# Second pass of a wavelet mixing kernel: smaller matmul tiles, two copies of the spread images, six places

## The chip, the cores and the metric

One Trainium2 chip, one core. The metric is the device time of the kernel in microseconds, lower is better. The kernel before takes 1980.73 us, the median of three runs.

## The reference

The input x is 8 batches of 32 channels, 256 images of 512x512 in float32. Each image is taken through a four-level wavelet analysis with symmetric padding. At the last level the low band and the three detail bands are 42x42 coefficients each; their channels are mixed, one 32x32 matrix for every coefficient, and the image is put together again. Only the last level is changed by the mix:

```
yl, yh = _dwt2(x, 4)
yl_out = einsum('bixy,ioxy->boxy', yl, w_yl)
yh_out = yh[:-1] + [einsum('bicxy,iocxy->bocxy', yh[-1], w_yh)]
return _idwt2(yl_out, yh_out)
```

Since the other levels come back as they were, the output is x plus the synthesis of the change in the 84x84 last-level coefficients (2 bands per axis, BANDS, of 42, COEFS; ROWS is 84). The kernel computes that.

## The kernel before, in words

**Pass 1** (to about 664 us) reads all 256 images, 1 MB each, on SyncE's queue (L325 to L333, eight slots) and brings each to 84x84 coefficients: TensorE along the height in 32x32 tiles (`h_stage`, L419), then a turn, then along the width. **The mix** (to about 739 us) goes over 32 pieces of weights (`mix`, L505 and L510, weights in a ring of four, L342); VectorE and ScalarE build its operands. In every four pieces TensorE also turns one step of the mixed coefficients of the last batch back, coefficients on partitions (`first_coefs`, L519), and ScalarE copies them to `delta` (`copy_delta`, L699).

**Pass 2** reads each image again, adds the synthesis of its delta and stores it. For an image ScalarE copies its 84x84 deltas to `pick` (L746); TensorE multiplies them with the width synthesis (the spread, L549, K=84 of 128 rows used, 512 columns, two records per float32 matmul); ScalarE copies the result to one of four `spread` buffers (L758); TensorE multiplies that with the height synthesis into PSUM banks 2 to 5 (the out stage, L565 for single images, L578 for pairs; four row sets k, each pair matmul 128 rows by 64 columns of the array and 512 long); VectorE adds PSUM to x in two halves (L854). TensorE waits for the add of the previous image's same half (`added`), and the add waits for `o_done`. The first 16 images, still on chip or loaded early, go singly; the other 240 as 120 pairs of 2 MB.

Three queues order pass 2. GpSimd's issues the loads (L302): a pair is loaded into place k of seven (`PLACES`, 2 MB each) once the pair stored from it has landed (`pair_stored`). SyncE's issues the stores in order (L370, L373, L377) once the adds are done. TensorE's order is written out: in `turn2` (eight images) the spread of image c+2 goes ahead of the out stage of image c. In every fourth `turn2`, seven times in all, the coefficients of the next batch are turned (`coefs_stage`, L539) between images, after ScalarE has staged them (`copy_stage`, L734) and before it copies them (`copy_delta`). The last pair is loaded and stored in pieces (L318, L380, L384).

## Time and profile before

| | |
|---|---|
| median of three runs | 1980.73 us (1978.71 to 1983.08) |
| the profiled execution | 1983.0 us, span 1981.1 us |
| TensorE matmul busy | 1899.7 us (96%) |
| VectorE, ScalarE, GpSimd busy | 825.3, 486.1, 72.7 us |
| moved | 558.29 MB read, 268.44 MB written, mean 418 GB/s |
| TensorE's granted clock, mean | 0.994 of full |

The span is what the profile of one core shows from its first to its last instruction. Busy shares are means over stages with different limits, and a busy TensorE is not one at its peak. DMA share is the mean busy share of the 16 DMA engines; it comes out a little above 1 where all 16 always have a packet.

### The profile page before, as it was taken

The numbers are of one execution on the slowest core, as the hardware profiler recorded it, in microseconds if no ns is written. First come the engines' busy times: TensorE is split into PE (matmuls) and PEld (weight loads), VectorE is DVE, ScalarE is ACT, GpSimd is POOL, SyncE is SP. The second block draws the span as 40 slices with busy tenths as digits, with TensorE's granted clock in tenths as the row PEclk, the third lists the DMA queues.
The fourth block names the chain that finished last, engine by engine and source line by source line (L and its number), as shares of the span: only waits on it lengthen the run. The fifth ranks groups of instructions, "written<-read, shape, count | busy, mean of one in ns | idle before, by whom it ended". The sixth has DMA issues, their size and how long they took to land.

```text
span 1981.1 us, 47583 instructions
## 1 busy us (share of the span) xinstructions
PE 1899.7 (96%) x19625; PEld 825.6 (42%) x19625; DVE 825.3 (42%) x931; ACT 486.1 (25%) x1060; POOL 72.7 (4%) x130
## 2 busy tenths in 40 slices
PE   8999999999999899999999999999999999999995
PEld 4666666666666554332232232232232232222221
DVE  2222222222222345555545555555545445445442
ACT  2233232332332551121121131121121121121110
POOL 1000000000000000000000000000000000000000
PEclk9999999999999999999999999999999999999998
DMA  9999999999999899999999999999999999999997
GB/s 383 405 408 414 412 422 421 421 422 422 422 422 422 338 406 381 420 421 430 429 430 429 431 429 431 430 431 430 430 429 429 430 431 431 430 431 431 430 432 303
DMA packets 80233, 827.12 MB, mean 418 GB/s; under 512 B 8912, under 2 KB 8912, under 8 KB 13520
## 3 DMA queue, kind: packets, MB, share of 16 engines
q1 hardware_dynamic: 62784, 575.10, 69.5%
q0 software_dynamic: 17424, 251.67, 29.9%
q8 instruction: 18, 0.29, 0.1%
q14 instruction: 7, 0.06, 0.0%
HBM read 558.29 MB, written 268.44 MB: 417 GB/s over the span
## 4 chain that ended last, share of the span: by engine, by line
PE 59%; DMA 36%; issue 2%; SPq 1%; DVE 1%; ACT 0%; DVEq 0%; POOLq 0%; ACTq 0%; POOL 0%
PE ps L578 27%; DMA x_sb<-x 19%; DMA out<-x_sb 16%; PE ps L419 10%; PE ps L549 8%; PE ps L432 5%; PE ps L565 3%; PE ps L510 1%; PE ps L505 1%; SPq L333 1%; PE ps L443 1%; DVE x_sb L854 1%; PE ps L451 1%; PE ps L539 1%; PE ps L465 1%
## 5 line engine op out<-in xcount | busy, mean ns | idle before, releaser
L854 DVE TENSOR_TENSOR x_sb<-ps,x_sb 128x1024 f32<-128x1024 f32 x292 | 354.9, 1223 | 348.4 <-PE ps L578 228.0
L578 PE MATMUL ps<-spread_sb,const 128*64 128x512 f32 x1920 | 438.9, 599 | 11.5 <-DVE x_sb L854 6.5
L578 PE MATMUL ps<-work,const 128*64 128x512 f32 x1920 | 438.9, 599 | 10.5 <-DVE x_sb L854 5.5
L854 DVE TENSOR_TENSOR work<-ps,work 128x1024 f32<-128x1024 f32 x220 | 267.3, 1223 | 255.9 <-PE ps L578 159.1
L419 PE MATMUL ps<-x_sb,const 32*32 32x512 f32 x8192 | 288.9, 601 | 23.1 <-DMA x_sb<-x 19.7
L549 PE MATMUL ps<-const,pick 128*84 128x512 f32 x514 | 277.1, 621 | 0.0
L432 PEld LDWEIGHTS ps<-const,work 128*128 128x128 f32 x2048 | 244.8, 192 | 51.8 <-ACT work L621 37.6
L578 PEld LDWEIGHTS ps<-spread_sb,const 128*64 128x64 f32 x1920 | 128.9, 138 | 312.8 <-issue 275.3
L578 PEld LDWEIGHTS ps<-work,const 128*64 128x64 f32 x1920 | 129.4, 139 | 311.3 <-issue 276.6
L432 PE MATMUL ps<-const,work 128*128 128x84 f32 x2048 | 253.9, 276 | 0.0
L621 ACT COPY work<-ps 128x512 f32<-128x512 f32 x256 | 131.4, 600 | 419.3 <-PE ps L419 419.3
L813 DVE COPY work<-ps 128x336 f32<-128x336 f32 x256 | 129.9, 507 | 151.2 <-PE ps L432 151.2
L419 PEld LDWEIGHTS ps<-x_sb,const 32*32 32x32 f32 x8192 | 138.8, 103 | 124.2 <-issue 85.0
L819 DVE COPY work<-ps 128x336 f32<-128x336 f32 x65 | 33.0, 507 | 342.0 <-PE ps L443 342.0
L758 ACT COPY spread_sb<-ps 84x512 f32<-84x512 f32 x121 | 70.3, 581 | 425.6 <-PE ps L549 424.8
L758 ACT COPY work<-ps 84x512 f32<-84x512 f32 x120 | 69.8, 581 | 417.1 <-PE ps L549 416.6
L549 PEld LDWEIGHTS ps<-const,pick 128*84 128x84 f32 x514 | 59.9, 151 | 185.8 <-issue 185.5
L302 POOL DMA_DIRECT2D x_sb<-x x68 | 36.2, 532 | 1383.2 <-DMA out<-x_sb 1383.2
L746 ACT COPY pick<-work 84x84 f32 (+1 forms) x258 | 67.3, 261 | 12.9 <-issue 10.4
L839 DVE COPY work<-mix_sb 32x448 f32<-32x448 f32 (+1 forms) x96 | 36.4, 379 | 37.4 <-PE ps L510 32.3
L443 PE MATMUL ps<-work,const 128*32 128x336 f32 x520 | 50.2, 458 | 0.6 <-DVE work L813 0.6
L451 PE MATMUL ps<-work,const 128*84 128x336 f32 x130 | 47.6, 448 | 0.6 <-DVE work L819 0.6
(46 smaller groups left out, 529.9 us busy)
## 6 DMA issues: line engine op xcount, KB each, us to landing
x_sb<-x SPq DMA_DIRECT2D x256, 1024.0 KB, 10.1
x_sb<-x POOLq DMA_DIRECT2D x68, 2048.0 KB, 16.5
out<-x_sb SPq DMA_DIRECT2D x68, 2048.0 KB, 38.2
work<-x POOLq DMA_DIRECT2D x51, 2048.0 KB, 16.5
out<-work SPq DMA_DIRECT2D x51, 2048.0 KB, 36.0
work<-w_full SPq DMA_DIRECT2D x30, 896.0 KB, 7.5
out<-x_sb SPq DMA_DIRECT2D x9, 1024.0 KB, 7.4
work<-x SPq DMA_DIRECT2D x8, 1024.0 KB, 6.3
```

What stands on the lines that cost most here:

```text
L419: last = nc.tensor.matmul(ps[to:to + TILE, m], const[part, A3H + TILE * r:A3H + TILE * r + TILE], x_sb[part, GROUP * a + m, r], start=r == ...
L432: last = nc.tensor.matmul(ps[:, 4 + m % 2, ROWS * k:ROWS * k + ROWS], along_h[:, m, P * k:P * k + P], const[:, A4 + ROWS * m:A4 + ROWS * ( ...
L443: last = nc.tensor.matmul(ps[TILE * k:TILE * k + TILE, 6, 0:GROUP * ROWS], const[:, at:at + TILE], turned[:, k].rearrange("p m r -> p (m r ...
L451: nc.tensor.matmul(ps[0:ROWS, 7, 0:GROUP * ROWS], const[:, A4:A4 + ROWS], third, start=True, stop=True).then_inc(c_done, 1)
L549: nc.tensor.matmul(ps[0:ROWS, p], pick[:, p], const[:, SW:SW + SIZE], start=True, stop=True).then_inc(s_done[p], 1)
L565: last = nc.tensor.matmul(ps[:, 2 + k], const[:, SH + P * k:SH + P * k + P], spread(c), start=True, stop=True)
L578: last = nc.tensor.matmul(ps[64 * h:64 * h + 64, 2 + k], const[:, SH + P * k + u:SH + P * k + P:2], spread(c - u + h), start=True, stop=True)
L621: nc.scalar.copy(along_h[:, m], ps[:, m]).then_inc(h_copied, 1)
L746: nc.scalar.copy(pick[0:ROWS, p], delta[0:ROWS, o]).then_inc(picked[p], 1)
L758: nc.scalar.copy(spread(c)[0:ROWS], ps[0:ROWS, p]).then_inc(s_copied[p], 1)
L813: nc.vector.tensor_copy(turned[:, :, m], ps[:, 4 + m % 2, 0:SEGS * ROWS].rearrange("p (k r) -> p k r", k=SEGS),).then_inc(t_copied, 1)
L854: nc.vector.tensor_tensor(part, ps[:, 2 + 2 * half:4 + 2 * half], part, ALU.add).then_inc(added[half], 1)
```

## The change

The synthesis of one half of an axis needs only 32 of the 42 coefficients of each band, so both products of pass 2 are cut in halves with K = 64. The spread of an image becomes 8 matmuls of 64x64 tiles, 256 columns each, into two PSUM banks; it is laid out twice, with the halves of the height on partitions 0 to 63 and 64 to 127 in both orders, and ScalarE copies both arrangements (eight buffers of 512 columns). The out stage of a pair image becomes 16 matmuls of 64x32 tiles, 512 long, the tiles of even and odd k on opposite rows of the array; of a single image 8 of 64x64. `pick` is written in two copies. A step of coefficients is turned by 8 matmuls without transpose mode in place of 4 with it, interleaved by band (`by_band`). The spread constants shrink from 1024 columns to 512. The places go from seven to six, and pass 2 is looped over groups of four images, `fours`. Turning the next batch now lies within one group of four, each step behind waits for the copies ahead of it. The cut diff (VectorE's loop over the places, SyncE's and the rest of ScalarE's group loop follow the same pattern and are left out):

```diff
-PLACES = 7
+PLACES = 6
 PAIRS = IMAGES // 2 - SLOTS
-ROUNDS2 = PAIRS // PLACES
-assert PAIRS == PLACES * ROUNDS2 + 1
+ROUNDS2 = PAIRS // PLACES - 1
+
+FOURS_BATCH = CHANNELS // GROUP
+FOURS = IMAGES // GROUP
+SINGLE = 2 * SLOTS // GROUP
+
+WINDOW, SHIFT = 32, COEFS - 32
...
-SW, SH, EYE, NEG = 592, 1104, 1616, 1744
+SW, SH, EYE, NEG = 592, 848, 1104, 1232
...
-    c[:ROWS, SW:SW + SIZE] = back.T
-    for r in range(ROW_RUN):
-        c[:ROWS, SH + P * r:SH + P * r + P] = back[r::ROW_RUN].T
+
+    windows = [[COEFS * b + SHIFT * h + j for j in range(WINDOW) for b in range(BANDS)] for h in range(2)]
+    for h in range(2):
+        part = slice(64 * h, 64 * h + 64)
+        half = back[SIZE // 2 * h:SIZE // 2 * (h + 1)]
+        assert np.abs(np.delete(half, windows[h], axis=1)).max() == 0
+        c[part, SW:SW + SIZE // 2] = half[:, windows[h]].T
+        for r in range(ROW_RUN):
+            of = h ^ (r % 2)
+            c[part, SH + 64 * r:SH + 64 * r + 64] = back[P * ROW_RUN // 2 * of + r:P * ROW_RUN // 2 * (of + 1):ROW_RUN, windows[of]].T
...
-        pick = sb("pick", [P, 2, ROWS])
-        spread_sb = sb("spread_sb", [P, 2, SIZE])
+        pick = sb("pick", [P, 2, P])
...
-        place += [work[:, e:e + 2 * IMAGE].rearrange("p (r w) -> p r w", w=SIZE) for e in (0, AT_W, AT_W + 2 * IMAGE)]
-
...
+        spreads = [AT_EARLY - SIZE] + [AT_EARLY + IMAGE + SIZE * e for e in range(6)]
+        assert max(at, AT_W + IMAGE * (EARLY - 3)) <= spreads[0]
+        spreads = [const[:, SW - SIZE:SW]] + [work[:, e:e + SIZE] for e in spreads]
...
-        def spread(c):
-
-            return spread_sb[:, c % 4] if c % 4 < 2 else more_spread[:, c % 4 - 2]
+        def spread(c, a):
+
+            return spreads[7 - (2 * (c % 4) + a)]
+
+        def by_band(step):
+
+            return step.rearrange("p (q j b) -> p q b j", q=Q, b=BANDS)
+
+        def window(rows, h):
+
+            return rows.rearrange("p (b r) -> p b r", b=BANDS)[:, :, SHIFT * h:SHIFT * h + WINDOW]
...
-            for k, e in ((4, 0), (5, 3), (6, 5)):
+            for k, e in ((4, 0), (5, 3)):
...
-            pool.wait_ge(pair_stored[0], 16 * ROUNDS2)
+            for k in range(PLACES - 1):
+                pool.wait_ge(pair_stored[k], 16 * ROUNDS2)
+                load_pair(k, PLACES * ROUNDS2 + k)
+            pool.wait_ge(pair_stored[PLACES - 1], 16 * ROUNDS2)
             for u in range(2):
-                pool.dma_start(place[0][:, 4 * u:4 * u + 4], x_pairs[0, :, 4 * u:4 * u + 4]).then_inc(last_loaded[u], 16)
+                rows = slice(4 * u, 4 * u + 4)
...
+            def turn_step(step, bank):
+
+                for q in range(Q):
+                    for h in range(2):
+                        last = nc.tensor.matmul(ps[64 * h:64 * h + 64, bank, P * q:P * q + P],
+                                                step[:, ROWS * q + 2 * SHIFT * h:ROWS * q + 2 * (SHIFT * h + WINDOW)],
+                                                const[:, EYE:EYE + P], start=True, stop=True)
+                return last
...
+            def coefs_stage(c, g, k):
+
+                pe.wait_ge(s_copied[c % 2], 2 * g + (c + 2) // 2 + 2)
+                for v in (2 * c, 2 * c + 1):
+                    pe.wait_ge(staged, STEPS * (k - 1) + v + 1)
+                    pe.sem_inc(d_begun, 1)
+                    turn_step(stage[:, v], 6 * (c % 2) + v % 2).then_inc(d_done, 1)
+
+            def spread_rows(p, of):
+
+                for a in range(2):
+                    for half in range(2):
+                        to = 64 * (half ^ a)
+                        for h in range(2):
+                            part = slice(64 * h, 64 * h + 64)
+                            last = nc.tensor.matmul(ps[to:to + 64, 6 * p + h, 256 * a:256 * a + 256], of(part, half),
+                                                    const[part, SW:SW + 256], start=True, stop=True)
+                last.then_inc(s_done[p], 1)
+
...
+                pe.sem_inc(s_begun, 1)
+                spread_rows(p, lambda part, half: pick[part, p, 64 * half:64 * half + 64])
+
+            def out_stage(c, g):
+
+                p, n = c % 2, GROUP * g + c
+                pe.wait_ge(s_copied[p], 2 * g + c // 2 + 2)
+                for two in range(2):
+                    pe.wait_ge(added[two], n + 1)
+                    pe.sem_inc(o_begun[two], 1)
+                    for k in (2 * two, 2 * two + 1):
+                        for half in range(2):
+                            at = 64 * (half ^ (k % 2))
+                            last = nc.tensor.matmul(ps[64 * half:64 * half + 64, 2 + k],
+                                                    const[at:at + 64, SH + 64 * k:SH + 64 * k + 64],
+                                                    spread(c, k % 2)[at:at + 64], start=True, stop=True)
+                    last.then_inc(o_done[two], 1)
+
+            def pair_stage(c, g):
+
+                u, n = c % 2, GROUP * g + c
                 for h in range(2):
-                    pe.wait_ge(s_copied[h], SLOTS // 2 * t + c // 2 + 2)
-                for half in range(2):
-                    pe.wait_ge(added[half], n + 1)
-                    for k in (2 * half, 2 * half + 1):
+                    pe.wait_ge(s_copied[h], 2 * g + c // 2 + 2)
+                for two in range(2):
+                    pe.wait_ge(added[two], n + 1)
+                    pe.sem_inc(o_begun[two], 1)
+                    for k in (2 * two, 2 * two + 1):
                         for h in range(2):
-                            last = nc.tensor.matmul(ps[64 * h:64 * h + 64, 2 + k], const[:, SH + P * k + u:SH + P * k + P:2],
-                                                    spread(c - u + h), start=True, stop=True)
-                    last.then_inc(o_done[half], 1)
-
-            def turn2(t, batch=None):
-
-                for c in range(SLOTS):
-                    if c < SLOTS - 2:
-                        spread_stage(c + 2, t)
+                            for half in range(2):
+                                at, to = 64 * (half ^ (k % 2)), 64 * h + 32 * half
+                                last = nc.tensor.matmul(ps[to:to + 32, 2 + k],
+                                                        const[at:at + 64, SH + 64 * k + u:SH + 64 * k + 64:2],
+                                                        spread(c - u + h, k % 2)[at:at + 64], start=True, stop=True)
+                    last.then_inc(o_done[two], 1)
...
+            def fours(g, batch=None):
+
+                for c in range(GROUP):
+                    if batch is not None and c >= 2:
+
+                        pe.wait_ge(d_copied, STEPS * batch + IDLE + 1 + 2 * (c - 1))
+                    if c < GROUP - 2:
+                        spread_stage(c + 2, g)
                     else:
+                        spread_stage(c + 2 - GROUP, g + 1)
+                    pair_stage(c, g)
+                    if batch is not None and c < STEPS // 2:
+                        coefs_stage(c, g, batch)
+                if batch is not None:
+                    pe.wait_ge(d_copied, STEPS * (batch + 1) + IDLE + 1)
+                    pe.sem_inc(d_begun, 1)
+
+            pe.wait_ge(cleared, 3)
+            spread_stage(0, 0)
+            with pe.Fori(0, SINGLE) as g:
+                for c in range(GROUP):
+                    if c < GROUP - 1:
+                        spread_stage(c + 1, g)
+                    else:
+                        spread_stage(0, g + 1)
+                    out_stage(c, g)
+            spread_stage(1, SINGLE)
+            with pe.Fori(SINGLE, FOURS_BATCH - 2) as g:
+                fours(g)
+            with pe.Fori(0, BATCH - 1) as k:
+                fours(FOURS_BATCH * k + (FOURS_BATCH - 2), batch=k + 1)
+                with pe.Fori(0, FOURS_BATCH - 1) as r:
+                    fours(FOURS_BATCH * k + r + (FOURS_BATCH - 1))
+            with pe.Fori(FOURS - 2, FOURS) as g:
+                fours(g)
...
+            def pick_image(c, g, single=False):
+
+                p, n = c % 2, 2 * g + c // 2
+                if single:
+                    o = CHANNELS - SLOTS - SLOTS * (g >> 1) + GROUP * (g & 1) + c
+                else:
+                    o = APART * ((g >> 3) & 1) + (CHANNELS - 2 - 2 * (c // 2) + c % 2) - GROUP * (g & (FOURS_BATCH - 1))
                 act.wait_ge(s_done[p], n)
+                for half in range(2):
+                    last = nc.scalar.copy(pick[:, p, 64 * half:64 * half + 64].rearrange("p (j b) -> p b j", b=BANDS),
+                                          window(delta[:, o], half))
+                last.then_inc(picked[p], 1)
+
+            def copy_spread(c, g, done):
+
+                p, n = c % 2, 2 * g + c // 2
                 act.wait_ge(s_done[p], n + 1)
+                act.wait_ge(o_done[1], done)
+                for a in range(2):
+                    last = nc.scalar.copy(spread(c, a).rearrange("p (h w) -> p h w", h=2),
+                                          ps[:, 6 * p:6 * p + 2, 256 * a:256 * a + 256])
+                last.then_inc(s_copied[p], 1)
+
+            def copy_spread_pair(c, g):
+                copy_spread(c, g, GROUP * g + (2 * (c // 2) - 1))
+
...
+            def fours(g, batch=None):
+                for c in range(GROUP):
                     if batch is not None and c == 0:
+                        for e in (2, 6, 7):
+                            act.wait_ge(early_stored[e], 16)
+                    if batch is not None and 1 <= c <= STEPS // 2:
+                        copy_delta(2 * (c - 1), batch, None)
+                        copy_delta(2 * (c - 1) + 1, batch, None)
+                    if c < GROUP - 3:
+                        pick_image(c + 3, g)
                     else:
+                        pick_image(c + 3 - GROUP, g + 1)
+                    if c < GROUP - 2:
+                        copy_spread_pair(c + 2, g)
                     else:
+                        copy_spread_pair(c + 2 - GROUP, g + 1)
+                    if batch is not None and c < STEPS // 2:
                         copy_stage(2 * c, batch)
                         copy_stage(2 * c + 1, batch)
+                if batch is not None:
+                    act.wait_ge(d_copied, STEPS * (batch + 1) + IDLE + 1)
```

## Rows read from the trace of the kernel before

**Rows 1.** The page: GB/s moved by DMA in 40 equal slices of 49.5 us.
```profile
GB/s 383 405 408 414 412 422 421 421 422 422 422 422 422 338 406 381 420 421 430 429 430 429 431 429 431 430 431 430 430 429 429 430 431 431 430 431 431 430 432 303
```
**Rows 2.** Windows: length, busy of PE, PEld, DVE, ACT, POOL, clock, DMA share, GB/s.
```profile
655.00:690.00 35.00, 28.94 (x1281) 20.43 (x1280) 15.34 (x39) 21.38 (x41) 0.00 (x0) 1.00 0.85 305
690.00:735.00 45.00, 42.26 (x2438) 27.75 (x2425) 23.36 (x61) 26.26 (x47) 0.00 (x0) 1.00 1.01 416
...
750.00:755.00 5.00, 5.00 (x13) 2.05 (x12) 2.75 (x3) 0.74 (x2) 0.00 (x0) 1.00 0.88 369
755.00:760.00 5.00, 5.00 (x13) 2.14 (x12) 3.16 (x3) 0.89 (x3) 0.66 (x1) 1.00 0.74 262
760.00:765.00 5.00, 5.00 (x13) 2.21 (x12) 2.67 (x3) 1.33 (x4) 0.00 (x0) 1.00 1.02 316
765.00:770.00 5.00, 5.00 (x13) 2.07 (x12) 2.45 (x2) 0.74 (x2) 0.00 (x1) 1.00 0.91 383
...
850.00:1500.00 650.00, 650.00 (x2616) 192.71 (x2614) 337.50 (x276) 140.99 (x337) 34.94 (x66) 1.00 1.01 430
1500.00:1950.00 450.00, 428.02 (x1693) 123.45 (x1689) 219.90 (x183) 84.04 (x206) 24.36 (x46) 1.00 1.01 431
```
**Rows 3.** Timeline, late in pass 2: start, length, engine, line, shapes, records [idle before <-releaser].
```profile
1512.41 3.66 PE L578 MATMUL ps<-spread_sb,const 128*64 128x512 f32 x16 [0.60 <-DVE work L854]
...
1516.00 1.09 PE L549 MATMUL ps<-const,pick 128*84 128x512 f32 x2
...
1520.99 2.35 DVE L854 TENSOR_TENSOR work<-ps,work 128x1024 f32<-128x1024 f32 x2 [3.65 <-DMA work<-x]
```
**Rows 4.** Groups by line and shape: records | busy us, mean ns | idle before.
```profile
L854 DVE TENSOR_TENSOR x_sb<-ps,x_sb 128x1024 f32<-128x1024 f32 x292 | 354.9, 1223 | 348.4 <-PE ps L578 228.0 <-DMA x_sb<-x 98.4 <-PE ps L565 22.0
...
L758 ACT COPY spread_sb<-ps 84x512 f32<-84x512 f32 x121 | 70.3, 581 | 425.6 <-PE ps L549 424.8
...
L746 ACT COPY pick<-work 84x84 f32 x224 | 58.5, 261 | 12.8 <-issue 10.4
...
L734 ACT COPY work<-mix_sb 128x336 f32 x36 | 27.2, 806 | 0.0
...
L699 ACT COPY work<-ps 84x512 f32 x30 | 16.3, 583 | 35.5 <-PE ps L539 35.0
```
**Rows 5.** Timeline in pass 1: two groups of 64 matmuls on 16 tiles.
```profile
79.42 4.46 PE L419 MATMUL ps<-x_sb,const 32*32 32x512 f32 x128 [0.46 <-DMA x_sb<-x]
...
90.50 5.96 PE L419 MATMUL ps<-x_sb,const 32*32 32x512 f32 x128 [1.61 <-DMA x_sb<-x]
```
**Rows 6.** Window over the second of these groups, columns as in rows 2.
```profile
92.00:96.00 4.00, 4.00 (x100) 2.04 (x91) 0.00 (x0) 0.00 (x0) 0.00 (x0) 0.68 1.01 422
```
**Rows 7.** Timeline from the mix into pass 2: last turn of coefficients, first stores.
```profile
739.25 0.64 PE L519 MATMUL ps<-const 128*84 128x128 f32 x4 [0.30 <-ACT const L690]
...
747.37 0.34 SPq L370 DMA_DIRECT2D out<-x_sb  x1
...
751.66 4.62 SPq L370 DMA_DIRECT2D out<-x_sb  x2
```
**Rows 8.** Waits from 690 to 740 us: who waited for what, total us, times, longest.
```profile
PEld ps L510 <- DMA work<-w_full: 12.2, 21, 1.2
```
**Rows 9.** The page's DMA issues: count, KB each, median us to landing.
```profile
x_sb<-x POOLq DMA_DIRECT2D x68, 2048.0 KB, 16.5
out<-x_sb SPq DMA_DIRECT2D x68, 2048.0 KB, 38.2
...
const<-consts SPq DMA_DIRECT2D x1, 592.0 KB, 12.2
```
**Rows 10.** The chain of waits at the end: start, length, what.
```profile
1892.45 45.14 DMA out<-x_sb
...
1938.55 21.36 DMA x_sb<-x
```
**Rows 11.** Window over the last stores, columns as in rows 2.
```profile
1967.00:1979.00 12.00, 0.00 (x0) 0.00 (x0) 0.00 (x0) 0.00 (x0) 0.00 (x0) 0.50 0.07 31
```

194 lines of the change are left out of this document (68 added, 126 removed).

## The prediction

> **What bounds the kernel now.** I read the slices first. TensorE is over 90% busy nearly everywhere, but so are the DMA engines, and their rate is the flatter of the two: 429 to 431 GB/s in every slice from about 900 us to 1930 us, 421 to 422 in pass 1, with one hole, 338, where pass 1 ends, and a shallow one, 381, where pass 2 begins [rows 1]. The windows then separate the two. From 850 to 1500 us TensorE is busy the whole time, from 1500 to 1950 it is idle 22 of 450 us, waiting through VectorE for loads; the DMA share is 1.01 in both and the rate 430 and 431 GB/s [rows 2]. So TensorE's being full or not makes no difference to what is moved. The chain of waits names the out stage for a large part of the span, but only because a full engine is never seen to wait. A pair is 2 MB in and 2 MB out, 4.19 MB, which at 431 GB/s is 9.73 us. TensorE needs 3.66 us for the out stage and about 1.0 for the spread, 4.7 an image and 9.3 a pair [rows 3], a little less than DMA: it is behind when pass 2 begins and has caught up by 1500 us.
>
> What a faster TensorE can win is thus only time in which DMA engines stand idle. There are three such places. From 655 to 690 us the share is 0.85: 5.3 us. From 750 to 770 us it is 0.88, 0.74, 1.02, 0.91 in four windows of 5 us, 0.12 + 0.26 + 0.09 = 0.47 of one, 2.35 us. By the rate (369, 262, 316, 383 against 430) it is (61 + 168 + 114 + 47) / 430 x 5 = 4.5 us [rows 2]. The third is the end: from 1967 to 1979 us the share is 0.07, one engine of sixteen (1/16 is 0.0625), still working through its stores [rows 11]. No matmul runs there, and the chain of the end is store 45.1 us, load 21.4 us, add, last store [rows 10].
>
> **The change part by part.**
>
> *The out stage and the spread.* Now 8 matmuls go two at a time in 3.66 us, 0.915 us for each round [rows 3]. In pass 1, 64 matmuls as long go sixteen at a time in 4.46 us, 1.115 us a round [rows 5]; there too four tiles of different rows write the same partitions in different banks, the pattern of the new code. The new out stage has 16 matmuls on eight tiles: two rounds, between 1.83 and 2.23 us. I take 2.0. The spread, 8 matmuls half as long on four tiles, is two rounds of half the length, 0.92 to 1.12, say 1.0. An image costs TensorE 3.0 us instead of 4.7, a pair 6.0 (5.5 to 6.7). VectorE's two adds of 1.22 us, 2.45 us an image [rows 4], and ScalarE's copies, 2 x 0.58 + 2 x 0.26 = 1.7 us instead of 0.84 [rows 4], both fit under it. All of it lies under the 9.73 us of DMA, so for the 120 pairs its worth is 0. The extra semaphore increments of TensorE lie there too.
>
> *The start of pass 2.* Single images now leave every 4.3 us (747.37 to 751.66) [rows 7], the 1 MB stores alone ask for 244 GB/s, and the loads of pairs only come once two stores have landed: that is the hole. With 3.0 us an image the stores ask for 350 GB/s. The first store comes later, however: the last turn of coefficients takes some 0.5 us more, image 0 needs its two picks (0.52), its spread is copied twice (0.58 more), and its first half out is shorter by 1.83 - 1.0 = 0.8. Instead of at 747.4 us [rows 7] it is issued at about 748.2, the second 3.0 us after it (4.3 now), and so on: by the eighth it is 8 us ahead of now. Up to about 752 DMA has early loads left, so the late start is covered. From then the stores and, from about 757, the loads fill it. Gain: between 0 and the 4.5 us of lost rate; I take the idle share, 2.3 us.
>
> *Turning coefficients in the mix.* Four matmuls take 0.64 us [rows 7]. Eight matmuls of 128 columns, each in two records and two at a time, are four rounds of a quarter of 0.915, 0.92 us at least; without overlap they are eight such rounds, 1.83. I take 1.15, 0.5 more, nine times. From 690 to 740 us TensorE waited for weights in 21 pieces, 12.2 us in all [rows 8], 2.3 us in four pieces, so the 0.5 there is hidden (at most 1.2, hidden as well). From 655 to 690 us DMA is not full, and two turns lie on the path: 1.0 us lost, 2.4 at most, 0 if ScalarE's copies end last there. The copies written with a stride of two elements read with a stride of eight as before (0.81 us); I cost them at nothing, as ScalarE was only 26 of 45 us busy [rows 2].
>
> *Constants.* The second load of constants was 592 KB [rows 9] for 1184 columns; 672 remain, 336 KB. 0.26 MB at 420 GB/s is 0.6 us of pass 1, where DMA is full. GpSimd's two memsets fewer are off the path.
>
> *Six places instead of seven.* In the cycle of a place the load takes 16.5 us and the store 38.2 to landing [rows 9], 54.7 us, or 5.6 pairs at 9.73 us: that many of the seven are in DMA's hands and the rest wait for or are in the adds. With six and a TensorE that no longer lags, about 0.6 of a place is with the engines and 5.4 in DMA. A transfer's own time at full rate is 4.9 us, so the queues are deep waits, not needed ones. Cost 0; what covers it is that depth. The slow sixteenth of DMA is the only thing that eats it: late in the run the store takes 45.1 us [rows 10]. GpSimd's queue waits for `pair_stored` as now and has nothing else behind; SyncE's stores keep their order.
>
> *The next batch's coefficients.* Seven times, within four images, ScalarE has 6 x 0.81 + 6 x 0.58 us more [rows 4] and TensorE six turns of 1.15. Were all serial, each image would take 4.5 + 5.3 = 9.8 us, the group 39 us against 19.5 of DMA: the adds fall 19.5 us behind, two pairs. 5.4 - 2 = 3.4 places are still in DMA. Cost 0 to 14 us (the rival below); I take 0, and TensorE regains 3.7 us a pair.
>
> *The end.* The last load still goes when a store has landed; the same two adds and last stores follow. 0.
>
> Sum: -2.3 - 0.6 + 1.0 = -1.9 us. The trace's own execution took 1983.0 us, 2.3 above the median of 1980.7, so it gives 1981.1 there and **1978.8 us** as a median. The bounds of the terms give -4.5 - 0.6 = -5.1 and 2.4 - 0.6 = +1.8.
>
> **The clock.** In pass 1 TensorE was idle for 1.6 us ahead of one group of 64 matmuls, the window over that group shows the clock at 0.68 in the mean, part of it at 1.2 GHz, and the group took 5.96 us instead of 4.46 [rows 5, 6]. Late in pass 2 it idles 0.6 us a pair at 2.4 GHz [rows 2, 3]; after the change it idles 9.7 - 6.0 = 3.7 us a pair. At half clock an image costs 6.0 us. With half of its work at 1.2 GHz a pair takes 9.0 us, still under 9.73, and the sum stays. With all of it there, 12.0, the kernel would be 2.3 us a pair slower; the threshold is 62% of the work at the low level, and an engine which is that full has been granted 2.4 GHz in this trace [rows 2]. The Trainium skill, "TensorE: Matmul & The Clock Gate", section "HAM oscillation — how this bites in real kernels", speaks against the change: matmuls in bursts with waits for DMA between them fall back to the low clock each time. By the row I expect this partly and at no cost.
>
> **The rivals.**
> - *The slow DMA engine is let go* (faster). One engine ends some 12 us after the rest [rows 11]. If its lag came from competition with fifteen full ones, six places would hold those back and it would catch up: up to 12 us less, 1967 to 1975, say 1971. For it: the lag is there. Against: when alone it moves 31 GB/s for the core, no more than a sixteenth of 431 (27) and a little. Chance 0.09.
> - *TensorE bounded after all until 1500 us* (faster). Then DMA would rise above 430 GB/s; 1% over 650 us is 6.5 us, 1974. Against: 430 with TensorE full, 431 with it waiting. Chance 0.05.
> - *Six places run dry at the next batch's coefficients* (slower). The group of four is the most serial part, and the slow engine's late landings (45.1 us instead of 38.2) take another 0.7 place. It decides from when the adds are some three pairs, 29 us, behind. At 2 us dry in each of seven places it is +14, 1993. Against: the estimate is 19.5 us with nothing overlapped. Chance 0.09.
> - *Tiles on different rows don't run at once, or the clock stays low* (slower). Four rounds for the out stage as now and 1.83 for the spread make 11.0 us a pair, 1.3 over DMA, 120 times: +150. Pass 1's sixteen tiles speak against it. Chance 0.03.
> - *The change doesn't do what it says*: the hole at 750 us stays, since landings and not issues space the loads there. 1981. Chance 0.08.
>
> **How the numbers follow.** The forecast has 0.66. About 0.2%, 4 us, is what a measurement of this kernel can tell from none: faster means under 1976.8, slower over 1984.7. Three runs scattered by 4.4 us, so a forecast of -1.9 with bounds -5.1 to +1.8 comes out faster in some 0.22 of its cases and slower in 0.04. Faster: 0.66 x 0.22 + 0.09 + 0.05 = 0.28. Slower: 0.66 x 0.04 + 0.09 + 0.03, rounded to 0.15. Same: 0.57. The range reaches from 1971.5, half of the slow-engine case, to 1985.5, the upper bound with scatter; left out are the slower cases and the other half, under 0.2.
>
> **What would show it.** TensorE's busy time in pass 2 near 3.0 us an image, VectorE then waiting for loads from about 900 us on instead of 1500, DMA share 1.01 and 430 GB/s from 760 to 1950 us as before, the windows from 750 to 770 us at 1.0, those from 655 to 690 a little lower than 0.85. I am wrong if a window after 850 us falls under 0.98, or if the last engine's tail is gone.

## The result, and the profile after

The changed kernel takes 2013.5 us (median of 4 runs, 2011.1 to 2017.1) against 1980.5 us before (1978.7 to 1983.1): 1.0167 times as long, 95% interval 1.0155 to 1.018. The forecast was 1978.8 us, no change. (The 1980.73 us ahead of the prediction was the median of the first three of the four runs before.) The profiled spans are 2015.3 and 1981.1 us, 34.2 apart.

Of the page of the changed kernel, its engines and the slices of 50.4 us, against [rows 1]:
```profile
span 2015.3 us, 65865 instructions
...
PE 1648.0 (82%) x27817; PEld 798.5 (40%) x27817; DVE 812.5 (40%) x931; ACT 644.9 (32%) x1579; POOL 71.1 (4%) x128
...
PEclk9999999999999999888988888888798888888787
DMA  9999999999999899999999999999999999999997
GB/s 382 413 413 421 419 421 422 422 422 422 422 422 421 328 397 417 426 430 431 430 430 426 424 427 420 407 395 403 405 415 405 410 409 411 414 402 411 409 414 294
```
TensorE is less busy, the DMA engines are as busy as before, and yet they move less: 430 GB/s until about 1050 us as before, then 420 to 427 and from about 1260 us 395 to 415. The changed kernel also executes 65865 instructions where the one before has 47583.

Its windows, columns as in [rows 2]:
```profile
655.00:690.00 35.00, 28.79 (x1343) 20.50 (x1344) 15.46 (x40) 20.01 (x38) 0.00 (x0) 1.00 0.82 292
...
750.00:755.00 5.00, 5.00 (x64) 2.41 (x60) 4.34 (x5) 2.39 (x8) 0.00 (x0) 1.00 1.01 423
755.00:760.00 5.00, 5.00 (x64) 2.40 (x59) 4.61 (x4) 2.38 (x8) 0.66 (x1) 1.00 1.00 359
760.00:765.00 5.00, 5.00 (x68) 2.54 (x64) 4.50 (x4) 2.38 (x9) 0.53 (x1) 1.00 0.99 403
765.00:770.00 5.00, 4.96 (x67) 2.40 (x63) 4.26 (x5) 2.63 (x8) 0.00 (x0) 1.00 1.03 434
...
850.00:1500.00 650.00, 484.62 (x6520) 162.33 (x6512) 305.19 (x256) 204.88 (x560) 33.94 (x64) 0.86 1.00 419
1500.00:1950.00 450.00, 328.75 (x4436) 109.55 (x4432) 209.93 (x178) 135.25 (x376) 23.34 (x44) 0.85 1.00 409
```
The hole at 750 us is filled, as forecast. The loss is below it: at 419 instead of 430 GB/s 650 us lose 650 x 11/430 = 16.6 us, at 409 instead of 431 450 us lose 23.0; 39.6 us in all, of which the gains below give some back. DMA's share is 1.00 in both windows (0.98 from 1300 to 1400 us), so hardly anything is seen to wait: the same transfers take longer.

The timeline of the changed kernel, late in pass 2, against [rows 3]: a spread, then an out stage at each of the clock's two levels.
```profile
1509.06 1.09 PE L584 MATMUL ps<-const,pick 64*64 64x256 f32 x16
...
1510.09 1.95 PE L623 MATMUL ps<-work,const 64*32 64x512 f32 x32
...
1517.11 3.67 PE L623 MATMUL ps<-work,const 64*32 64x512 f32 x32 [4.05 <-DVE x_sb L924]
```
The DMA issues on its page, against [rows 9]:
```profile
x_sb<-x POOLq DMA_DIRECT2D x80, 2048.0 KB, 22.1
out<-x_sb SPq DMA_DIRECT2D x80, 2048.0 KB, 32.0
```
Load and store together are 54.1 us from issue to landing (54.7 before), but of six places now, not of seven: six pairs at the 9.73 us of before are 58.4 us, and 4.3 us of slack are left of 13.4.

The DMA view of two windows of 4 us of the changed kernel, its two large queues (q0 GpSimd's with the loads of pairs, q1 SyncE's with the stores; packets, MB, share of 16 engines). From 1504 to 1508 us:
```profile
q1 hardware_dynamic: 95, 1.56, 105.0%
q0 software_dynamic: 7, 0.07, 3.9%
```
From 1509 to 1513 us:
```profile
q0 software_dynamic: 92, 1.51, 96.6%
q1 hardware_dynamic: 10, 0.08, 4.9%
```
The same view of the kernel before, 1500 to 1505 us:
```profile
q0 software_dynamic: 70, 1.11, 52.0%
q1 hardware_dynamic: 68, 1.05, 49.0%
```
Loads and stores used to be mixed at every moment; now they come in turns. In the trace's DMA records a 16 KB packet took 0.611 us in the mean of 1600 to 1900 us before and 0.641 after, 4.9% more, which is the missing rate. The turns are not shown to be what slows the packets. Take the difference between load and store packets in bins of 2 us, as a share of their sum, from 1600 to 1900 us: it is 0.12 before, 0.65 after, 0.20 in e2 below, and e2's packets took 0.629 us all the same.

**One engine falls behind.** In the trace the store of a pair has 16 landings, and I take each for one of the 16 DMA engines; where one lags, it fits the tail of [rows 11] with one sixteenth of DMA busy. I call the time between the first and the last of a pair's 16 store landings the *spread of a store*. Before, it grows from 3.8 us (at 982 us) to 28.7 (at 1948), most of it between the last landing and the others (22.0): one engine loses 24.9 us in 966, 2.6%, which ends as the 12 us of [rows 11]. After the change it grows from 9.9 us (952) to 21.5 (1195), 4.8%, and stays at 24 to 26 from about 1250 us on. The stay is where the rate falls.

The table is worked out from the traces of all kernels but e9 and e14: matmuls in pass 2 for each pair image, places, growth of the spread with its end points, the level at which it stays, and the time against the kernel before. The times of landings here, in the table and with every spread below are counted from the start of the recording, some 10 us ahead of the span's start from which windows and slices count. Each growth is from one trace.
```
run     matmuls  places  growth (us at us)                level  ratio [95% interval]
before     9       7     2.6% (3.8@982, 28.7@1948)         -     1
after     24       6     4.8% (9.9@952, 21.5@1195)         25    1.0167 [1.0155, 1.018]
e1         9       6     2.2% (3.4@972, 24.6@1917)        (25)   1.0013 [1.0003, 1.0023]
e2        24       7     5.4% (9.2@933, 31.8@1355)         36    1.0085 [1.0068, 1.0102]
e3        24       5     -                                 17    1.0123 [1.0105, 1.0142]
e4         9       7     2.9% (4.7@981, 32.3@1948)         -     1.0004 [0.9994, 1.0013]
e5         9       4     -                                  5    1.006  [1.0041, 1.008]
e6         9       7     2.7% (4.7@978, 30.5@1945)         -     0.9991 [0.9978, 1.0004]
e7        36       6     6.5% (10.3@965, 26.0@1208)        26    1.0194 [1.0163, 1.0226]
e8        24       6     5.8% (9.7@954, 23.8@1196)         26    1.0128 [1.0089, 1.0168]
e10       17       7     3.8% (3.3@979, 35.2@1815)         35    1.0052 [1.0036, 1.0069]
e11        9 +96   7     13.8% (7.9@925, 39.3@1152)        40    1.0593 [1.0573, 1.0613]
e12       24       6     5.4% (9.1@956, 22.3@1199)         26    1.0136 [1.0114, 1.0158]
e13        9 +48   7     10.6% (7.4@917, 38.6@1211)        39    1.0394 [1.0351, 1.0437]
e15       19       6     4.2% (6.8@961, 21.8@1320)         25    1.0067 [1.005, 1.0083]
e16        5       7     1.5% (5.0@981, 19.1@1941)         -     0.9978 [0.9962, 0.9994]
e17        9 +24   7     3.4% (6.6@982, 32.5@1746)         35    1.0025 [1.0011, 1.0038]
e18       19       7     3.9% (5.5@848, 24.4@1336)         36    1.0078 [1.0054, 1.0103]
(+n: n instructions more on SyncE for each pair, as the trace counts them)
```

**Where each kernel loses.** The DMA records also say how much later a kernel has moved the same bytes than the kernel before. What this delay grows by from 850 to 1950 us is the loss in the pair stage alone: 40 us in the change, 0 in e1, 18 in e2, 35 in e3, 11 in e5, 0 in e6, 36 in e7, 25 in e8, 4 in e10, 107 in e11, 30 in e12, 68 in e13, 13 in e15, 2 in e17, 13 in e18, and e16 gains 1. The rest of a difference in time arises where pass 2 begins or in the last 50 us.

### The profile page after: what moved, and what is told of

It reads as the page before. It is cut to its first block, busy times and chain, and to the rows that moved or that the text cites. A ratio compares the mean times of both kernels' runs of the same rounds, so it can differ in the third digit from the quotient of the medians.

```text
span 2015.3 us, 65865 instructions
## 1 busy us (share of the span) xinstructions
PE 1648.0 (82%) x27817; PEld 798.5 (40%) x27817; DVE 812.5 (40%) x931; ACT 644.9 (32%) x1579; POOL 71.1 (4%) x128
## 4 chain that ended last, share of the span: by engine, by line
DMA 65%; PE 27%; DVE 3%; issue 2%; SPq 1%; ACT 1%; DVEq 0%; ACTq 0%; POOLq 0%; POOL 0%
DMA x_sb<-x 31%; DMA out<-x_sb 26%; PE ps L450 10%; DMA out<-work 5%; PE ps L463 5%; DMA work<-x 4%; PE ps L623 3%; DVE x_sb L924 2%; PE ps L541 2%; PE ps L536 1%; PE ps L606 1%; PE ps L584 1%; SPq L359 1%; PE ps L474 1%; PE ps L549 1%
## 5 line engine op out<-in xcount | busy, mean ns | idle before, releaser
L623 PE MATMUL ps<-work,const 64*32 64x512 f32 x6720 | 577.9, 706 | 297.2 <-DVE x_sb L924 199.1
L924 DVE TENSOR_TENSOR x_sb<-ps,x_sb 128x1024 f32<-128x1024 f32 x336 | 400.1, 1221 | 429.8 <-DMA x_sb<-x 340.4
L810 ACT COPY work<-ps 128x512 f32<-128x512 f32 x450 | 244.8, 589 | 803.8 <-PE ps L584 802.5
L623 PEld LDWEIGHTS ps<-work,const 64*32 64x32 f32 x6720 | 122.8, 114 | 591.7 <-issue 591.6
L584 PE MATMUL ps<-const,pick 64*64 64x256 f32 x4128 | 320.1, 430 | 2.2 <-issue 2.2
L924 DVE TENSOR_TENSOR work<-ps,work 128x1024 f32<-128x1024 f32 x176 | 209.3, 1220 | 230.3 <-DMA work<-x 174.1
L623 PE MATMUL ps<-const 64*32 64x512 f32 x960 | 280.2, 698 | 0.0
L584 PEld LDWEIGHTS ps<-const,pick 64*64 64x64 f32 x4128 | 151.0, 148 | 292.3 <-issue 266.8
L676 ACT COPY work<-ps 128x512 f32<-128x512 f32 x256 | 131.4, 599 | 416.7 <-PE ps L450 416.7
L800 ACT COPY pick<-work 128x64 f32 (+1 forms) x518 | 105.2, 261 | 12.6 <-DMA out<-work 12.4
L549 PE MATMUL ps<-const,work 128*64 128x128 f32 x672 | 44.0, 286 | 13.9 <-ACT work L788 13.7
```

The lines of the kernel that those rows point to most:

```text
L549: last = nc.tensor.matmul(ps[64 * h:64 * h + 64, bank, P * q:P * q + P], step[:, ROWS * q + 2 * SHIFT * h:ROWS * q + 2 * (SHIFT * h + WIND ...
L584: last = nc.tensor.matmul(ps[to:to + 64, 6 * p + h, 256 * a:256 * a + 256], of(part, half), const[part, SW:SW + 256], start=True, stop=True)
L623: last = nc.tensor.matmul(ps[to:to + 32, 2 + k], const[at:at + 64, SH + 64 * k + u:SH + 64 * k + 64:2], spread(c - u + h, k % 2)[at:at + 6 ...
L676: nc.scalar.copy(along_h[:, m], ps[:, m]).then_inc(h_copied, 1)
L800: last = nc.scalar.copy(pick[:, p, 64 * half:64 * half + 64].rearrange("p (j b) -> p b j", b=BANDS), window(delta[:, o], half))
L810: last = nc.scalar.copy(spread(c, a).rearrange("p (h w) -> p h w", h=2), ps[:, 6 * p:6 * p + 2, 256 * a:256 * a + 256])
```

## The experiments

The letters in the expectations are the theories of the moment; each is spelled out there. A diff shows the lines that carry the edit, the rest of it is left out.

**e1, six places alone.** The kernel before with `PLACES = 6` and the last round's loads and stores as the change has them.
```diff
-PLACES = 7
+PLACES = 6
```


> The kernel before with one edit: six places for pairs in place of seven. Theory A (depth): one of the 16 DMA engines falls behind, each place is held until its last sixteenth has landed, and with six places the other fifteen run out of stores and then of loads by turns, which slows each packet; then this kernel is slower than before by 1.0 to 1.7%, 2000 to 2015 us, its DMA rate falls from 430 to about 410 GB/s somewhere after 1050 us, loads then take some 22 us and stores 32. Theory B (pace and traffic): it is the new tiles, the adds that follow each load at once, the half clock or ScalarE's doubled copies that disturb DMA; then this one stays within 0.2% of before.


1985.9 us, +0.13%. Its page:
```profile
GB/s 367 415 419 421 413 416 423 416 422 422 420 422 422 329 405 382 392 417 425 431 429 431 431 429 429 430 431 432 430 431 431 430 432 430 431 431 430 431 429 316
```
430 GB/s to the end: the number of places alone is not it. Its few us are lost where pass 2 begins: the slices from 743 to 893 us have 382, 392 and 417 GB/s, those of [rows 1] 381, 420 and 421, 3.7 us.

**e2, the new tiles with seven places** (to make room, the stage of coefficients is halved, an early image lies elsewhere, and the first 16 images use two spread buffers instead of four).
```diff
-PLACES = 6
+PLACES = 7
```


> The changed kernel with seven places (room is made by a ring of four steps for the staged coefficients, by an early image under spread buffers, and by two spread buffers in place of four for the first 16 images). Theory A (depth): 1976 to 1981 us, -0.2 to 0.0%, DMA at 430 GB/s to the end. Theory B (pace and traffic): as slow as the changed kernel, 2005 to 2015 us.


2000.5 us, +0.85%: half of the loss. Its page:
```profile
GB/s 367 412 419 421 419 422 422 422 422 422 422 422 421 305 394 416 423 425 431 428 428 427 430 428 428 428 428 424 428 424 415 418 418 414 420 420 414 421 410 272
```
The rate falls only from about 1500 us on, after the spread has reached 36 us instead of 25. With the old tiles and six places the pair stage loses nothing (e1), with the new tiles and seven places 18 us, with both changes 40.

**e3, five places.** As the change, with one place fewer.
```diff
-PLACES = 6
+PLACES = 5
```


> The changed kernel with five places. Theory A (depth): slower still than with six: the fifteen engines run dry earlier, before 900 us, and have less to do by turns; 2030 to 2100 us, and the DMA share falls under 0.98. Theory B (pace and traffic): within 0.3% of the changed kernel.


2008.9 us, less than with six. The level is 17 us, reached about 1130 us. So the levels go 17, 25, 36 with five, six, seven places, about a pair's time (9.7 us) apart, but the loss does not grow with each place taken.

**e4, queues swapped.** Before, with the pair loads on SyncE and all stores of pass 2 on GpSimd.
```diff
-                    pool.wait_ge(pair_stored[k], 16 * i)
-                    load_pair(k, PLACES * i + k)
+                    pool.wait_ge(added[1], 2 * PLACES * i + (2 * SLOTS + 2 * k + 3))
+                    pool.dma_start(out_pairs[i * -PLACES + (PAIRS - 1 - k)], place[k]).then_inc(pair_stored[k], 16)
```


> The kernel before with its seven places, but in pass 2 GpSimd's queue issues all stores and SyncE's all loads of pairs. It asks where the slow sixteenth comes from. If it belongs to GpSimd's queue, the lag now shows in the stores' landings as before but more strongly, or at the loads not at all; if it belongs to one engine whatever the queue, time and the tail of some 12 us at the end stay: within 0.3% of before. If the lag goes, the tail does, and it is 8 to 12 us faster.


No change, and the spread grows by 2.9% all the same. The Trainium skill ("DMA: Bandwidth & Descriptors", section "Latency and other measured facts") says that two of the sixteen engines are usually slower and guesses at the descriptor rings of GpSimd's path. In these traces there is one, and it doesn't care which queue does what. GpSimd's queue is still in use in e4, so the guess itself is not tested.

**e5, four places.** Before, the last round as in e1.
```diff
-PLACES = 7
+PLACES = 4
```


> The kernel before with four places. Theory A2: one engine's lag can only grow as far as the places let it (stores landed 17, 25 and 36 us apart at most with five, six and seven places of the new tiles); once it is at that cap, the other fifteen engines load and store by turns and their packets slow down, with whatever tiles. With four places the cap is some 8 us, which the old tiles' lag reaches by about 1200 us: 2005 to 2025 us, DMA under 420 GB/s from there on. Theory B2: only a TensorE that is well ahead of DMA brings the alternation; the old tiles keep 430 GB/s after 1200 us, and the loss is under 0.5%.


1996.8 us, +0.6%. Its page:
```profile
GB/s 376 419 417 420 418 421 422 422 422 422 422 422 421 329 399 379 313 407 430 431 430 431 430 427 424 427 423 420 428 425 420 429 425 423 428 426 422 428 427 387
```
The spread stays at 5 us from about 1190 us on, and from there the rate is 420 to 429 GB/s: 11 us are lost between 850 and 1950 us. With few enough places the old tiles do, more weakly, what the new ones do with six. But the +0.6% is not that loss. With only four places pass 2 begins with a hole (313 GB/s in the slice from 797 us, where the kernel before has 420; 12 us), and at the end the small spread gives some 10 us back (387 GB/s in the last slice, 303 before). Neither theory had these two.

**e6, half the columns.** Before; the last matmuls compute only the left half of 240 images. TensorE then has the idle time and the sagging clock (0.916) of the changed kernel.
```diff
-                                                    spread(c - u + h), start=True, stop=True)
+                                                    spread(c - u + h)[:, 0:256], start=True, stop=True)
```


> The kernel before with seven places whose pair stage multiplies only 256 of the 512 columns, so that TensorE needs some 2.9 us an image with the old tiles and ScalarE's copies stay single. Left out: the right half of the synthesis of 240 images. Theory B2 (pace): as slow as the new tiles with seven places, 1993 to 2003 us, with slow packets and alternation late in the run. Theory C (traffic of the new tiles: more weights, more instructions, two copies): 1976 to 1982 us.


0.9991 [0.9978, 1.0004]: with the old tiles and seven places, a fast TensorE with idle time and a lower clock costs nothing.

**e7, padded.** The change with half of the out stage's matmuls and every second spread issued twice, so that TensorE is nearly as full as before (91% busy against 96%).
```diff
-                    for k in (2 * two, 2 * two + 1):
+                    for k in (2 * two, 2 * two + 1) * (2 - two):
```


> The changed kernel, six places, with TensorE's work padded by repeated matmuls (the first two row sets of the out stage twice, every second spread twice) to about 4.5 us an image, 9.0 a pair, the pace of the kernel before. Theory B2 (pace): back to 1980 to 1988 us, packets at full rate. Theory C (traffic): 2005 to 2020 us.


2024.2 us, 1.0194 [1.0163, 1.0226] with the clock at 0.99, and the change 1.0167 [1.0155, 1.018]: no better, nor clearly worse. In the pair stage it loses 36 us, the change 40; the rest is where pass 2 begins, at the old pace. Pace with more matmuls is no remedy.

**e8, one copy.** The change without the second arrangement of the images: the matmuls read the first in its place.
```diff
-                for a in range(2):
+                for a in range(1):
```


> The changed kernel, six places, ScalarE copies each spread image once instead of twice and all row sets read that one copy. Left out: the second arrangement, so odd row sets get the wrong halves. If the doubled copies disturb DMA's reads of on-chip memory: 1985 to 2000 us. If not (theories A2 and B2): within 0.3% of the changed kernel, 2008 to 2019 us.


1.0128 [1.0089, 1.0168], growth 5.8%: ScalarE's copies are at most a small part.

**e9, increments on TensorE.** e6 with 30 semaphore increments for each image.
```diff
+                for _ in range(30):
+                    pe.sem_inc(idle, 1)
```


> The old tiles with half the columns (1982 us), with 30 more semaphore increments on TensorE's queue for each pair image: as many more instructions as the new tiles have, with no more data read on chip. Left out: the right half of the synthesis of 240 images. Theory C1 (instruction stream): the stores' lag grows at 5% of the time instead of 3%, reaches its cap of some 36 us before the end, and the time is 1990 to 2003 us. Theory C2 (what the new matmuls read on chip disturbs DMA): 1979 to 1985 us, lag growth 3%.


2335.8 us, and nothing learned: the increments made TensorE the bound, loads landed in 11 us, and no engine could fall behind.

**e10, the same work in more matmuls.** Before, each last matmul split into two of 256 columns. No semaphore and no other tile; the weight loads of these matmuls double with them.
```diff
-                        for h in range(2):
-                            last = nc.tensor.matmul(ps[64 * h:64 * h + 64, 2 + k], const[:, SH + P * k + u:SH + P * k + P:2],
-                                                    spread(c - u + h), start=True, stop=True)
+                        for w in range(0, SIZE, SIZE // 2):
+                            for h in range(2):
+                                last = nc.tensor.matmul(ps[64 * h:64 * h + 64, 2 + k, w:w + SIZE // 2],
+                                                        const[:, SH + P * k + u:SH + P * k + P:2],
+                                                        spread(c - u + h)[:, w:w + SIZE // 2], start=True, stop=True)
```


> The kernel before, seven places, each pair matmul of 512 columns cut into two of 256: the pair stage's instructions and weight loads double, the data it streams stays. Theory C1: lag growth near 5%, 1990 to 2005 us. Theory C2, if it is the streamed data: 1979 to 1986 us; if it is the weight loads, as under C1.


1991.3 us, +0.5%: 7680 instructions more (55263), growth 3.8% instead of 2.6, the level of 35 us reached at about 1800. Much of the loss is at the very end, where the slow engine works on alone for longer: the last slice of 50 us has 265 GB/s, 303 before, which is 4.4 us.

**e11, more instructions on SyncE**, which otherwise only waits and issues stores.
```diff
                     sp.dma_start(out_pairs[i * -PLACES + (PAIRS - 1 - k)], place[k]).then_inc(pair_stored[k], 16)
+                    for _ in range(96):
+                        sp.sem_inc(idle, 1)
```


> The kernel before with 96 semaphore increments on SyncE's queue behind each store of a pair. If any engine's instructions slow one DMA engine (C1, general): lag growth over 4%, 1985 to 2000 us. If only TensorE's do, or none: within 0.3% of before.


2097.7 us, +5.9%. Stores still take 50.6 us to landing, so DMA and not SyncE is the bound; one engine loses 13.8%. But the DMA view shows SyncE's own code arriving, which it does 7 times in the kernel before:
```profile
q14 instruction: 124, 1.02, 0.1%
```
The packets come in every round of seven pairs, some seven of 8 KB in each of the 17 rounds; in the kernel before, the rounds go by without them. So e11 mixes two things.

**e12, the new tiles at half the columns.** As e6, on the changed kernel: the right half of 240 images is left out.
```diff
-                                last = nc.tensor.matmul(ps[to:to + 32, 2 + k],
+                                last = nc.tensor.matmul(ps[to:to + 32, 2 + k, 0:256],
```


> The changed kernel, six places, pair stage over 256 of the 512 columns: all its instructions and weight loads stay, the streamed data halves. Left out: the right half of the synthesis of 240 images. Theory C1: within 0.3% of the changed kernel, 2008 to 2019 us. Theory C2: 1990 to 2003 us.


1.0136 [1.0114, 1.0158]: little comes back with half the streamed data, as many instructions and a clock of 0.87.

**e13, waits instead of increments.** e11 with waits that are long fulfilled.
```diff
-                        sp.sem_inc(idle, 1)
+                        sp.wait_ge(t_done, 1)
```


> The kernel before, with 96 waits on a semaphore that has long reached its value issued by SyncE behind the store of every pair, in the place where e11 had 96 increments. Nothing else waits for them, and no semaphore is written. The theory that the mere number of instructions that the engines fetch slows one DMA engine (I) expects the same as e11: 2080 to 2110 us, the store's first and last landing apart by a growing time, some 14% of time. The theory that it is the writing of semaphores (S) expects the kernel before: 1978 to 1984 us, apart by 3% of time.


2059.4 us, +3.9%, growth 10.6%. The trace has two waits as one instruction: 5712 more, 48 for each pair, half of e11's. No semaphore is written, so the writing is not the cause. The code is loaded again here too:
```profile
q14 instruction: 90, 0.74, 0.1%
```

**e14, the increments in a loop.**
```diff
+                    with sp.Fori(0, 24) as _:
+                        for _ in range(4):
+                            sp.sem_inc(idle, 1)
```


> The kernel before, with the 96 increments of e11 executed by SyncE as 24 turns of a loop of four. As many semaphore writes as e11, but the code is short and each turn repeats it. If the cost lies in bringing straight-line code to the engine (I with short loops kept near the engine): near the kernel before, 1978 to 1990 us. If it lies in executing increments (S), or if each turn of a loop is fetched anew: 2080 us or more, the latter with more than e11 for the loop's own register and branch instructions.


2325.9 us: the loop's own instructions seem to have made SyncE the bound (at 1511 and 1524 us its stores leave 12.8 us apart, where a pair took 9.7). Loads landed in 11.2 us and no spread built up. It answers nothing.

**e15, the new tiles with fewer matmuls.** The spread of an image is three matmuls over block-diagonal constants instead of eight: 19 instead of 24, the output the same. The constants are 256 columns wider, and TensorE is fuller again: 90% busy, clock 0.99.
```diff
-                            last = nc.tensor.matmul(ps[to:to + 64, 6 * p + h, 256 * a:256 * a + 256], of(part, half),
-                                                    const[part, SW:SW + 256], start=True, stop=True)
+                    last = nc.tensor.matmul(ps[to:to + 64, 6 * p + 1], of(slice(0, P), half),
+                                            const[:, SW:SW + SIZE], start=True, stop=True)
```


> The changed kernel, but the spread of an image is three matmuls over block-diagonal constants of 512 columns instead of eight small ones: 19 instead of 24 matmuls an image, the output as before. Instruction theory (I): a third of what the change added goes, so the DMA lag grows a little slower and the time falls to between 2000 and 2011 us. A theory that the tiles' form or the second copy costs it (F): 2010 to 2016 us, as the changed kernel.


1997.7 us, +0.67%: more than half of the loss is back, more than was expected. Its page:
```profile
GB/s 383 411 406 419 420 421 422 422 421 422 420 422 418 317 392 375 418 427 428 429 430 430 428 427 431 430 430 429 422 423 420 421 423 418 422 424 414 423 425 307
```
The rate holds until about 1400 us, where the spread reaches 25, and then falls less, to some 421 (the change: 409). Part of the 0.67% is not this fall: the hole where pass 2 begins is back (375 GB/s in the slice from 749 us; the change 417). In the pair stage e15 loses 13 us where the change loses 40.

**e16, half the last matmuls.** Before; the rows of one image of each pair are left out.
```diff
-                        for h in range(2):
+                        for h in range(1):
```


> The kernel before with four of the eight last matmuls of each pair left out (the rows of one image of each pair are not synthesised; its output there is not the reference's). Instruction theory (I): fewer instructions than before, so the DMA lag grows by less than 3% of time and the time falls by 2 to 8 us, to 1973 to 1979 us. If the 3% of the kernel before is a property of the DMA engine and not of the instructions: 1979 to 1983 us and the lag as before.


1977.4 us, 0.9978 [0.9962, 0.9994], growth 1.5%. The gain is in the tail: the last slice of 49 us has 340 GB/s, 303 before, 4.2 us. The lag of the kernel before comes at least partly from its instructions too.

**e17, few increments.** e11 with a quarter of them.
```diff
-                    for _ in range(96):
+                    for _ in range(24):
```


> The kernel before with 24 increments by SyncE behind each pair's store, a quarter of e11. e11's and e13's traces hold 124 and 90 packets of SyncE's code where the kernel before has 7, because a round of seven pairs was longer than what the engine keeps; here it should be short enough. If every executed instruction slows one DMA engine (I): a quarter of e11's, the lag grows by some 4 to 6% of time instead of 3, 1984 to 1995 us. If in e11 and e13 only the repeated loading of code did it (R): 1979 to 1983 us, lag 3%. If the code is still loaded each round (packets of SyncE's code would show it): 2000 us or more, and the two can't be told apart.


1986.6 us, 1.0025 [1.0011, 1.0038], growth 3.4%. SyncE's code is loaded as often as before, but for one packet:
```profile
q14 instruction: 8, 0.07, 0.0%
```
So instructions that are only executed make the engine lose time as well. The 0.25% is small: 2 us in the pair stage and 3.5 in the last slice (273 GB/s, 303 before). Per instruction e17's growth is less than a third of e11's and e13's, where code is loaded again; that the loading makes this difference is likely, not shown.

**e18, both remedies.** e15 with seven places, as in e2.
```diff
-PLACES = 6
+PLACES = 7
```


> The new tiles with both remedies: seven places (e2) and the spread in three matmuls (e15), output as before. If the lag and its cap are the whole loss (I): growth 4.2% of time from about 850 us as in e15, cap 36 us as in e2, reached at about 1700 us, so 1984 to 1990 us, ratio 1.002 to 1.005, better than either remedy alone. If the two remedies act on the same thing and don't add, or the new tiles cost something else: 1993 us or more. Faster than the kernel before (under 1978 us) is expected by neither.


1999.4 us, +0.78% (1992.8 to 2001.6): no better than e15 alone, and the expectation fell. Its page:
```profile
GB/s 381 409 407 421 420 421 422 417 422 422 422 422 421 313 390 379 425 428 427 431 430 427 429 428 430 430 424 422 420 421 427 429 426 417 428 416 421 421 423 270
```
The rate drops to between 416 and 429 at about 1300 us, though the spread is then 24 us and its level of 36 comes at about 1800. From 1370 us a second engine is late as well (at 1406 us the last landing of a store stands 13.5 us behind the one before it, at 1336 us 17.9, while the spread grew from 24.4 to 27.3). What does that is open.

## Why the prediction was wrong

**The step that failed** is "Six places instead of seven. ... Cost 0; what covers it is that depth", together with "for the 120 pairs its worth is 0" of the out stage and spread. I had added up depth in times to landing and counted 0.6 of a place for the engines; I had seen the slow engine (45.1 against 38.2 us, and the tail of [rows 11]) and taken it for a fixed property of 12 us at the end. It is a rate. An engine that loses g of its time is invisible in the rate as long as the others can run ahead of it. A place is loaded again only when all sixteen have stored, so they can run ahead by what the places allow: 17, 25 or 36 us with five, six or seven (39 and 40 in e13 and e11). After that the slow engine holds the others back. If the core then went at the slow engine's pace, the changed kernel would move 430 x (1 - 0.048) = 409 GB/s, and the last window shows 409. The time lost would be g times what is left of the run: (2015 - 1250) x 0.048 = 37 us. From there to 1950 us it did lose 38.

This agreement is better than the rule behind it. The same sum gives for the others, with the loss of the pair stage behind it: e1 2 (0), e17 5 (2), e10 7 (4), e15 at 1400 us 25 (13), e2 at 1440 us 30 (18), e12 at 1200 us 44 (30), e8 at 1200 us 47 (25), e7 at 1210 us 53 (36), e13 at 1215 us 89 (68), e11 at 1155 us 130 (107). It is too high for all of them, in the larger ones by a fifth to nearly a half, and has e12, e8 and e7 above the change, which loses more than each. From 1600 to 1900 us their rates fall by only half to four fifths of g (418 GB/s in e2 where the rule gives 407, 411 in e12 for 407, 415 in e8 for 405). e18 (13 us where it gives some 7) it misses on the other side. So that the lag and its level bring the loss is shown; how much of the lag comes through is not explained. A larger lag also lengthens the tail at the end, by some 4 us in e10 and e17.

What g goes with is, in this kernel, the number of instructions. For each pair image 5 matmuls go with 1.5%, 9 with 2.2 to 2.9 (four traces), 17 with 3.8, 19 with 3.9 and 4.2, 24 with 4.8 to 5.8 (four traces), 36 with 6.5, and 24 instructions of an otherwise idle SyncE for each pair add 0.8 to the 2.6 of the kernel before. Among matmuls this can't be told from their weight loads; SyncE's instructions have none. Nothing in the change's arithmetic is at fault, only that 64-row tiles need 24 matmuls where 9 did, and that one place fewer lets their price be seen some 200 us earlier (at 1250 instead of e2's 1440). That pair of causes is shown (e1, e2, e10, e15, e16, e17). Against the rivals speak single runs: e6 and e12 against idle time, clock and streamed data, e4 against the queues, e8 against the copies (1.0128 [1.0089, 1.0168] without half of them); e7 brings back the pace, but with more matmuls. e15 has fewer matmuls and nearly the pace and clock of before at once, so that a part of its gain may be the pace's. e10, e16 and e17 have only the number changed. Kernels alike in matmuls and places still differ: the change, e12 and e8 lose 40, 30 and 25 us in the pair stage.

How an instruction costs a DMA engine time is not shown. Every run here lists its granted clock, so every run was recorded; the Trainium skill ("NOTIFIC — the notification-queue block", its opening) says that instruction tracing writes 16-byte records into rings in memory. No run here tells whether the lag comes from the instructions or from such records of them, and none was made without a recording.

**TensorE's pace**: right. The out stage takes 1.95 us at full clock (forecast 2.0), the spread 1.09 (1.0), a turn of coefficients 1.09 (1.15).

**The start of pass 2**: right in kind. The shares 0.88, 0.74, 1.02, 0.91 of [rows 2] became 1.01, 1.00, 0.99, 1.03. By the rate 7 + 71 + 27 - 4 = 101 GB/s are missing over the four windows, 1.2 us instead of 4.5: a gain of 3.3 (2.3 forecast). The first store went at 746.54 us (748.2 forecast, 747.37 before).

**Turning coefficients in the mix**: not settled. The share from 655 to 690 us fell from 0.85 to 0.82, 0.03 x 35 = 1.05 us (1.0 forecast), but e1, with the old turn, has 0.81 there, and e2, with the new one, 0.74. From 690 to 735 us, where the prediction had the cost hidden, the rate is 403 GB/s where it was 416, 1.4 us, with the share at 1.01 in both.

**The clock**: right that it would fall partly and cost nothing. It is 0.86 in the mean from 850 us on; at half clock an out stage takes 3.67 us, and e6 (clock 0.916, time 0.9991) shows that it need not be in the time. The prediction weighed the Trainium skill ("TensorE: Matmul & The Clock Gate", section "HAM oscillation — how this bites in real kernels"), where bursts of matmuls with waits for DMA between them fall back to the low clock each time. This trace agrees in part: the clock falls 67 times between 850 and 1950 us, while some 110 pairs go by.

**Constants, the next batch's coefficients, the end**: all hidden or small as forecast; in the windows from 850 to 1000 us, before the spread is used up, the rate is 430 GB/s through a batch boundary. The 5.3 us an image that the prediction adds for the next batch is too much by its own terms: 6 x (0.81 + 0.58 + 1.15) = 15.2 us are 3.8 for each of four images. This helps its conclusion.

**The rivals.** "The slow DMA engine is let go" had the right engine and the wrong sign: I supposed that holding the fifteen back would help the sixteenth. It doesn't catch up, it slows them. "Six places run dry" (+14) had the right side and place, priced for a burst at seven batch boundaries instead of a loss at every pair. No rival had a cost that grows with the number of instructions. The condition that I gave for being wrong, a share under 0.98, was too weak: the share stayed at 1.00, in two windows of 50 us at 0.98, while packets took 4.9% longer. The rate was the thing to name. The other condition, that the tail is gone, did not come: from 2009 to 2012 us the share is 0.06, one engine of sixteen.

No version here is faster than the kernel before with its whole output; the 0.2% of e16 is bought with output left out, and it shows about what four matmuls fewer could bring to it.

## What to carry to other kernels

Where DMA is the bound, read the spread of a transfer's landings over the run: if it grows with one landing far behind the rest, one engine is slower, and the buffers in flight, not the mean time to landing, say how long that stays hidden. Then a buffer given up and instructions added cost more together than each alone: here one place fewer cost 0.13% (nothing of it in the pair stage), the new tiles 0.85%, both 1.67%. And look at where a difference arises before you give it a cause: e1's, e5's and e16's were not where they were looked for, but at the start of pass 2 or in the tail. A faster TensorE bought with 2.7 times as many matmuls is no gain when nobody waits for it.

## What the runs showed of the hardware that was not expected

- A DMA share of 1.00 is no measure of rate: from 1600 to 1900 us 16 KB packets took 0.611 us before and 0.641 after the change, at 431 and 409 GB/s.
- 24 instructions on SyncE for each 9.7 us, with nobody waiting for them, cost 0.25% and took one DMA engine's loss from 2.6 to 3.4%; 96 of them, with their code loaded again each round, 5.9% and 13.8%. All of it was seen with the recording on.
